# Cross-attention and feed-forward kernel: four tiles' residual sums moved to ScalarE and GpSimd, and the first block's carry, counts and stores set later

## The reference

```python
def rmsnorm(x, g):  return x * rsqrt(mean(x*x) + 1e-5) * g

h  = rmsnorm(layernorm(x), g_res) @ W_in + b_in               # 4096 x 512 by 512 x 512
p  = rmsnorm(context, g_init)[:, :512]                        # 3202 rows
s  = scan over rows: s[r] = a * s[r-1] + b * p[r]             # a, b constants
x1 = x + h + s[clip(cumsum(boundary_mask) - 1)]               # rows of s, gathered
out = x1 + gelu(layernorm(x1) @ w1 + b1) @ w2 + b2            # hidden size 2048
```

## Time and profile before

| | before |
|---|---|
| median of 3 runs | 831.66 us (831.65 to 832.69) |
| profiled execution, its own time | 834.93 us |
| its span in the profile | 833.2 us |
| TensorE busy | 822.3 us, 99% |
| VectorE, ScalarE, GpSimd busy | 315.9, 294.0, 258.0 us |
| granted TensorE clock | 1.0 in all 40 slices |
| first stage ends (last projection's end) | at about 118.2 us |

### The profile page before, as it was taken

How to read it: one execution, slowest core, us unless ns; L and a number is a source line. 1 busy time by engine, 2 the same in 40 slices (tenths; PEclk the granted TensorE clock), 3 DMA queues, 4 the chain that set the end, 5 groups by cost and what they waited for, 6 DMA issues and landing times.

```text
span 833.2 us, 10703 instructions
## 1 busy us (share of the span) xinstructions
PE 822.3 (99%) x3722; PEld 675.9 (81%) x3722; DVE 315.9 (38%) x513; ACT 294.0 (35%) x542; POOL 258.0 (31%) x238
## 2 busy tenths in 40 slices
PE   7999999999999999999999999999999999999998
PEld 5877878788888888888888888888888888888886
DVE  5899852665141423233332423143113411241112
ACT  5668446422622253224422262222222222222221
POOL 2254659940633035301630062305300250011000
PEclk9999999999999999999999999999999999999999
DMA  9988994260236022602233113302300240010001
GB/s 227 281 263 282 291 301 153 89 163 22 68 102 160 0 76 88 167 7 74 72 113 80 50 58 103 50 0 101 51 1 1 79 72 0 0 50 1 1 0 51
DMA packets 39057, 78.11 MB, mean 94 GB/s; under 512 B 6369, under 2 KB 6369, under 8 KB 37265
## 3 DMA queue, kind: packets, MB, share of 16 engines
q1 hardware_dynamic: 30052, 65.95, 24.3%
q0 software_dynamic: 4608, 8.39, 6.4%
q10 hardware_dynamic: 4368, 3.42, 1.5%
HBM read 51.02 MB, written 22.84 MB: 89 GB/s over the span
## 4 chain that ended last, share of the span: by engine, by line
PE 81%; POOL 7%; DVE 4%; DMA 3%; issue 2%; SPq 1%; ACT 1%; ACTq 0%; POOLq 0%; DVEq 0%
PE acc L889 13%; PE acc L890 13%; PE acc L891 13%; PE h_bank L889 13%; PE h_bank L890 13%; PE h_bank L891 13%; DMA xa_odd<-in_x_dram 2%; POOL w_lo L545 2%; PE t_bank L948 2%; POOL x_cur L651 1%; POOL x_next L577 1%; DMA scan_table<-cl_next 1%; POOL cl L564 1%; POOL w_lo L551 1%; DVE h_lo L1070 1%
## 5 line engine op out<-in xcount | busy, mean ns | idle before, releaser
L1303 DVE TENSOR_TENSOR h_lo<-g_f,h_hi 128x512 fp32r<-128x512 f32 x128 | 101.1, 790 | 432.1 <-ACT g_f L826 432.1
L824 ACT ACTIVATE h_hi<-h_bank,b_c 128x512 fp32r<-128x512 f32 x128 | 87.9, 687 | 429.5 <-PE h_bank L891 425.9
L889 PE MATMUL h_bank<-xt_hi,w_hi 128*128 128x512 f32 x512 | 199.9, 390 | 0.6 <-POOL w_lo L545 0.6
L889 PE MATMUL acc<-w_hi,h_hi 128*128 128x512 f32 x512 | 199.8, 390 | 0.0
L891 PE MATMUL h_bank<-xt_hi,w_lo 128*128 128x512 f32 x512 | 199.3, 389 | 0.0
L890 PE MATMUL h_bank<-xt_lo,w_hi 128*128 128x512 f32 x512 | 199.2, 389 | 0.0
L891 PE MATMUL acc<-w_hi,h_lo 128*128 128x512 f32 x512 | 199.2, 389 | 0.0
L890 PE MATMUL acc<-w_lo,h_hi 128*128 128x512 f32 x512 | 199.2, 389 | 0.0
L889 PEld LDWEIGHTS h_bank<-xt_hi,w_hi 128*128 128x128 f32 x512 | 96.1, 188 | 20.7 <-issue 1.0
L891 PEld LDWEIGHTS h_bank<-xt_hi,w_lo 128*128 128x128 f32 x512 | 96.1, 188 | 20.0
L891 PEld LDWEIGHTS acc<-w_hi,h_lo 128*128 128x128 f32 x512 | 96.1, 188 | 20.0
(11 more groups left out here) (168 smaller groups left out, 701.1 us busy)
## 6 DMA issues: line engine op xcount, KB each, us to landing
out_dram<-x_cur SPq DMA_DIRECT2D x32, 256.0 KB, 2.1
x_next<-x_part SPq DMA_DIRECT2D x7, 1024.0 KB, 5.0
w_raw<-in_L_ffn_w_dram SPq DMA_DIRECT2D x6, 1024.0 KB, 9.0
scan_table<-cl SPq DMA_DIRECT2D x6, 896.0 KB
ch<-in_ctx_dram SPq DMA_DIRECT2D x20, 256.0 KB, 2.9
cl<-in_ctx_dram SPq DMA_DIRECT2D x5, 1024.0 KB
xa_odd<-in_x_dram SPq DMA_DIRECT2D x16, 256.0 KB, 7.3
x_part<-xa_odd SPq DMA_DIRECT2D x16, 256.0 KB, 3.9
```

Source lines behind the costliest of these rows:

```text
L824: act.activation(h_hi[:, m % HB, :], h_bank[m % 2][:], ACT.Gelu, bias=b1_c[:, m:m + 1])
L889: nc.tensor.matmul(dst, a_hi, b_hi, start=first, stop=False)
L1303: dve.tensor_tensor(h_lo[:, m % HB, :], g_f32[:], h_hi[:, m % HB, :].bitcast(F32), ALU.subtract).then_inc(h_split, 1)
```

## The change

It touches the first stage only. It has these parts:

- `HOSTED` begins at 16, so that tiles 16 to 19 also come turned from DRAM. They take the places (`w_raw`, quarter 3) that tiles 28 to 31 have afterwards; the loads of those four are issued at t = 21 and 22, and wait for `x_lo`.
- `BY_POOL` = (13, 15, 17, 19): the sums of these tiles are made by ScalarE (`scale_sums`: bank times `ra` into a half of `ch`) and GpSimd (`add_scaled`: that plus x), at step t + 1. VectorE's `tile_add` of them is gone, and TensorE waits for `sums_scaled` to use their banks again.
- Statistics of tiles 21 and 23 go from ScalarE to VectorE.
- `carry(0)` goes from t = 15 to 16 on TensorE and `count_positions` from 16 to 17. On VectorE the halves of `add_carry(0)` go from t = 15 and 16 to 16 (behind the scans) and 17, and `count_rows` from t = 17 to 18, behind `add_carry(1)`. `carry(1)` and `count_before` stay at t = 19 and 20.
- SyncE stores block 0 at t = 17 and not 16; block 1 is stored at t = 18 in both.

```diff
-STORE0 = 16
+STORE0 = 17
-ON_ACT = (6, 8, 10, 18, 20, 21, 22, 23, 24, 25, 26, 27)
+ON_ACT = (6, 8, 10, 18, 20, 22, 24, 25, 26, 27)
+BY_POOL = tuple(range(13, 20, 2))
+BY_DVE = tuple(t for t in range(NT) if t not in BY_POOL)
-HOSTED = tuple(range(20, NT))
+HOSTED = tuple(range(16, NT))
+PLACES = 12
...
-            q = 1 + u // K
+            q = (3, 1, 2, 3)[u // K]
...
             def store_x1(t):
-                wait_apart(sp, acc_read, t + 1)
+                if t in BY_POOL:
+                    wait_apart(sp, pool_added, BY_POOL.index(t) + 1)
+                else:
+                    wait_apart(sp, acc_read, BY_DVE.index(t) + 1)
...
-                if 5 <= t < 5 + len(HOSTED) // 2:
-                    for u in (2 * (t - 5), 2 * (t - 5) + 1):
+                if 5 <= t < 5 + PLACES // 2 or t in (21, 22):
+                    for u in (2 * (t - 5), 2 * (t - 5) + 1) if t < 21 else (2 * (t - 15), 2 * (t - 15) + 1):
+                        if u >= PLACES:
+                            wait_apart(sp, x_lo, HOSTED[u - PLACES] + 1)
                 if t == STORE0:
                     store_block(0, cl)
-                if t == STORE0 + 2:
+                if t == STORE0 + 1:
                     store_block(1, cl_next)
...
+            def add_scaled(t):
+                n = BY_POOL.index(t)
+                pool.wait_ge(sums_scaled, n + 1)
+                pool.tensor_tensor(xa(t), xa(t), ch[:, n % 2, :], ALU.add).then_inc(pool_added, 1)
+
             for t in range(NT):
+                if t - 1 in BY_POOL:
+                    add_scaled(t - 1)
...
+            def scale_sums(t):
+                n = BY_POOL.index(t)
+                act.wait_ge(h_used, t + 1)
+                act.wait_ge(ra_ready, t + 1)
+                if n >= 2:
+                    act.wait_ge(pool_added, n - 1)
+                u = t % XR
+                act.activation(ch[:, n % 2, :], p_bank[t % 3][:], ACT.Copy, scale=ra[:, u:u + 1]).then_inc(sums_scaled, 1)
...
                     tile_high(t + 2)
+                if t - 1 in BY_POOL:
+                    scale_sums(t - 1)
...
-                if t == 15:
+                if t == 16:
                     pe.wait_ge(consts_made, 5)
                     carry(0, cl, acc[3][:])
-                if t == 16:
+                if t == 17:
                     count_positions()
...
-                if t > 0:
+                if t > 0 and t - 1 in BY_DVE:
                     tile_add(t - 1)
...
                 if t == 15:
-                    add_carry(0, acc[3][:], cl, (0, 1))
                     scan_row(1, cl_next, 1)
                 if t == 16:
-                    add_carry(0, acc[3][:], cl, (2, 3))
                     scan_row(1, cl_next, 2)
                     scan_row(1, cl_next, 3)
+                    add_carry(0, acc[3][:], cl, (0, 1))
                 if t == 17:
-                    count_rows()
+                    add_carry(0, acc[3][:], cl, (2, 3))
                 if t == 18:
                     add_carry(1, acc[3][:], cl_next, (0, 1))
                     add_carry(1, acc[3][:], cl_next, (2, 3))
+                    count_rows()
```

More of the change, by code:

```diff
@@ L98, in left @@
         self.n = self.entered + turns * self.per
-ON_ACT = (6, 8, 10, 18, 20, 21, 22, 23, 24, 25, 26, 27)
+ON_ACT = (6, 8, 10, 18, 20, 22, 24, 25, 26, 27)
 ON_DVE = tuple(t for t in range(NT) if t not in ON_ACT)
+BY_POOL = tuple(range(13, 20, 2))
+BY_DVE = tuple(t for t in range(NT) if t not in BY_POOL)
+ND = len(BY_DVE)
 def stats_made(tiles, t):
     return sum(1 for v in tiles if v < t)
-HOSTED = tuple(range(20, NT))
+HOSTED = tuple(range(16, NT))
+PLACES = 12
 def xattn_ffn(nc, x, x_cols, ctx, mask, w_in, b_in, g_res, g_init, w1, b1, w2, b2, out):
@@ L319, in xattn_ffn @@
         acc_read = sem("acc_read")
+        sums_scaled = sem("sums_scaled")
+        pool_added = sem("pool_added")
         w_hi_done = sem("w_hi_done")
@@ L345, in xattn_ffn, with wait_read @@
         block = es.enter_context(nc.Block())
+        def wait_read(engine, t):
+            if t in BY_POOL:
+                engine.wait_ge(sums_scaled, BY_POOL.index(t) + 1)
+            else:
+                engine.wait_ge(acc_read, BY_DVE.index(t) + 1)
         def block_start(b):
@@ L447, in _ @@
                     store_block(0, cl)
-                if t == STORE0 + 2:
+                if t == STORE0 + 1:
                     store_block(1, cl_next)
                 if t == 22:
+                    wait_apart(sp, pool_added, len(BY_POOL))
                     load_high_half(NA, 0)
@@ L456, in _ @@
                 if t == 29:
-                    wait_apart(sp, x_lo, HOSTED[K])
+                    wait_apart(sp, x_lo, HOSTED[2 * K])
                     load_w1(1)
@@ L462, in _ @@
             store_x1(NT - 1)
-            wait_apart(sp, x_lo, HOSTED[2 * K])
+            wait_apart(sp, x_lo, HOSTED[3 * K])
             load_w1(2)
@@ L488, in group @@
                 for i in range(TI):
-                    wait_apart(sp, acc_read, NT + TI * g + i + 1)
+                    wait_apart(sp, acc_read, ND + TI * g + i + 1)
                     sp.dma_start(out_v[g, :, i, :], x_cur[:, i, :]).then_inc(out_stored, 16)
@@ L895, in project @@
                 if t >= 3:
-                    pe.wait_ge(acc_read, t - 2)
+                    wait_read(pe, t - 3)
                 for k in range(K):
@@ L990, in _ @@
                 project(t)
-            pe.wait_ge(acc_read, NT - 2)
+            pe.wait_ge(acc_read, ND - 2)
             pe.wait_ge(block_ready, NA)
@@ L1012, in ffn2 @@
                 if m == 0:
-                    pe.wait_ge(acc_read, NT + TI * g)
+                    pe.wait_ge(acc_read, ND + TI * g)
                 if m < 12:
```

## The result

The changed kernel takes 834.59 us in the median of 7 runs (834.39 to 836.03), the kernel before 831.65 us beside it (831.57 to 833.3): +2.94 us, a ratio of 1.0035 with a 95% interval of 1.0024 to 1.0045. It is slower by 0.35%. That is 1.0 us beyond the forecast of 833.6, just outside the forecast's own 832.5 to 834.5 us and inside the whole range of 831.5 to 835.0. Its profiled execution took 836.03 us, with a span of 834.1.

The account below looks back on a forecast made before the run. TensorE was taken as the bound: despite 1.84 us saved, VectorE makes `count_before` 2.6 us late, less 0.65 given back, net 1.95 us, so the median goes from 831.66 to 833.6 us. Own range 832.5 to 834.5, whole range 831.5 to 835.0 us.

Parts of the forecast that it names:

- The bound: TensorE, busy nearly the whole span: the change is worth how much group 0 shifts; nothing waits from t = 21 to 29.
- The chain on VectorE: VectorE from tile 17's low part, without blocking: 7.82 us to the end of `add_carry(0)`, 12.67 us to that of `count_rows`.
- The start of the low part: VectorE's low part of tile 17 begins 0.58 us later, at 69.97 us, behind ScalarE's `scale_sums(13)`.
- Blocking: VectorE's low parts of tiles 17, 19 and 20 lose 0.7 us each beside GpSimd's adds, 2.1 us in all.
- The wait ahead of `carry(1)`: At t = 19 TensorE waits about 2.4 us for VectorE's half carry.
- The wait ahead of `count_before`: At t = 20 TensorE waits 1.9 us for VectorE's counts.
- a sign of being wrong: If TensorE reaches `count_before` last, VectorE's chain is shorter than forecast and the prediction is wrong.
- Lateness: `count_before` on TensorE comes 2.6 us late, at 84.75 and not 82.16 us.
- What is given back: TensorE's 0.65 us wait for `n_rows` at t = 31 goes, leaving 1.95 us net.
- The base: Profiled execution of 834.93 us, 3.3 us above the median of the runs shown; 1.95 us is added to both.
- Blocking in full: Rival: each low part waits nearly all of a GpSimd add, 1.09 us; 3.15 us slower, 834.8 us; chance 0.13.
- The gathers come late too: Rival: block 1's rows land late behind block 0's store, the t = 31 wait stays; +2.4 us, 834.1 us; chance 0.10.

Follow-up runs that it names:

- e8: Changed kernel with the statistics of tiles 21 and 23 back on ScalarE; 834.17 us, ratio 1.0023 to the kernel before.
- e10: Changed kernel with GpSimd's four adds of scaled sums cut from 512 columns to 8; 834.52 us, ratio 1.0024 to the kernel before.
- e7: Changed kernel with the four sums back on VectorE; 834.54 us, ratio 1.0029 to the kernel before.
- e4: Kernel before with the later carry, counts and stores alone; 833.36 us, ratio 1.0014 to the kernel before.
- e12: e11 with the last three of GpSimd's bias adds moved from steps 15 to 17 to step 19; 832.28 us, ratio 0.9988 to the kernel before.
- e1: Kernel before, unchanged, run again for a second profile; 833.54 us in one run.
- e6: Kernel before with hosted columns from tile 16 alone; 832.45 us, ratio 1.0006 to the kernel before.
- e2: Changed kernel with `count_rows` ahead of `add_carry(1)` on VectorE; 835.98 us, ratio 1.0040 to the kernel before.
- e3: e2 with 20 unread transposes on TensorE filling the wait ahead of `carry(1)`; 835.46 us, ratio 1.0030 to the kernel before.
- e11: e6 with the statistics of tiles 14 and 16 moved from VectorE to ScalarE; 831.91 us, ratio 0.9997 to the kernel before.
- e9: e5 with GpSimd's four adds of scaled sums cut from 512 columns to 8; 834.44 us, ratio 1.0024 to the kernel before.
- e5: Changed kernel with the first block's carry, counts and stores back at their old steps; 836.45 us, ratio 1.0046 to the kernel before.

## Why the prediction was right

- **The bound.** "From t = 21 to 29 nothing waits", and nothing behind group 0 moves: 35.3 to 35.4 us from the counts to group 0 in eight profiles, 715.0 us behind in both kernels. Right.
- **The chain on VectorE.** Bare 7.82 us to the end of `add_carry(0)`: measured 7.78 (changed), 7.77 (e8: 77.24 - 67.78 - 1.69), 7.79 (e10), 7.87 (e7). Bare 12.67 to the end of the counts: 12.76. The step that gave the sign held to a tenth. The start of the low part, put 0.58 us later for ScalarE's scaled sum, was 0.65 later: 12.27 us behind step 13's transposes (68.79 - 56.52) against 11.62 in e4 (67.03 - 55.41).
- **Blocking.** 2.1 us forecast, 0.7 each; 0.75, 0.94 and 0.41 measured. That it was near the forecast as a sum is partly luck: e7, e10 and e12 show that which operation is hit, and how hard, changes with every shift.
- **The wait ahead of `carry(1)`.** 2.4 forecast, 2.38 measured.
- **The wait ahead of `count_before`.** 1.9 us forecast, none seen in the one profile; the time (1.74 us) was lost all the same, in a slower clock, which the prediction leaves out. In e8, at full clock, the wait is there. That TensorE came to the counts just with them was named as a sign of being wrong; it came of the clock, not of a shorter chain. Lateness 2.6 forecast, 2.5 measured.
- **What is given back.** "Then the wait of 0.65 us at t = 31 is gone": it went, but e1, e4 and e6 have none either, so it was nothing that these executions have to give. This is the mis-sized term: 0.65 us on the net of 1.95. With 0 the forecast would have been 834.3 us. Another 0.14 us lies outside the span: a run's time less its span is 1.90 us on average for the changed kernel, 1.76 for the one before. 2.5 + 0.14 = 2.6 of the 2.94 us; the rest, 0.3, stays open (the start of step 10 varies by 1.9 us between profiles, most of it with the low clock from 12 to 20 us).
- **The base.** "Stands 3.3 us above the median" was taken as an offset common to both. It was not: 1.97 us of it were waits of steps 11 to 13, which the changed kernel's profile did not have. The medians bore the forecast difference, the two profiles (1.1 us apart) didn't. The same waits were in both starting points of the sum, VectorE's 69.39 and TensorE's 82.16, and that they nearly cancel is luck. In e4, with the same order up to there and no late steps, the low part of tile 17 is 67.03 - 45.80 = 21.23 us behind step 10's transposes, not 69.39 - 45.81 = 23.58, which is 2.35 us less where TensorE has 1.97 less. The lateness should have been forecast 0.4 us smaller; three small terms gave it back (0.07 in the start of the low part, 0.09 in the chain, 0.14 from the end of the counts to TensorE's start).
- **Rivals.** "Blocking in full" had 834.8 us, nearer to 834.59 than the forecast, but not its mechanism: the low parts lost 2.10 us, not 3.3. "The gathers come late too" did not happen in the changed kernel (no wait for `n_rows`), but e2 and e3 show it 1 us behind, for another reason than the one given: not the block's store but the statistics of tile 23 ahead of GpSimd's scales.

What the pieces are worth, by the timed medians: hosted columns +0.6 us (not clear of no change) for a saving of 1.84; the moves alone +1.2; all together +2.9. The gain was not there to keep in this order of work, as VectorE is what TensorE waits for from step 15 to 19.

## What to carry to other kernels

When the bound engine has work taken off it, follow the engine next to it from the first place where it runs without a pause, row by row, before counting a gain: here 1.84 us saved became 2.0 us of new waits (e6). Between two engines that block each other's two-operand operations, an edit moves much of the blocked time rather than removing it (2.10 us in the changed kernel, 1.63 without the four adds, 1.10 with them cut to 8 columns; 1.7 in e11 and 2.3 in e12); three sums of 128x8 cost 0.6 or 2.5 us by where they fall. Before a wait is booked as "given back", look whether a second execution of the same kernel has it, and measure differences from a row behind the start.

## What the runs showed of the hardware that was not expected

- The same idle time of TensorE, 2.37 to 2.54 us, was followed by 1.2 GHz in two profiles (changed, e10) and by the full clock in two (e2, e8); around 3.38 us of it the clock was 0.54 and 0.61 in two stretches of 4 us (e7). The same at the start: a wait of 1.9 to 2.0 us that ends near 13 us was followed by a clock below 1.00 in four profiles (changed, e9, e10, e11) and by the full clock in two (e5, e6); waits of 1.4 to 1.7 us there were followed by the full clock in all eight others.
- A tiny operation loses as much as a long one: the first of three 128x8 sums took 1.05 us in e12 and the third 1.19, where 0.17 is usual, and the three lost 1.88 us. Halves of a carry, with a bank as one operand, lost nothing beside adds (1.28 us at 77.06 in the changed kernel).
- GpSimd loses too: an add of 8 columns took 1.94 us in e9 behind VectorE's 1.88 us of one-hot rows, an add of 512 columns 3.03.
